# The next group's layer norm and step sizes beside the state steps, its denominators at the head of the pairs

## The reference, cut to what matters

```python
proj = x @ W_in.T
z, xc, dt_raw, bc = jnp.split(proj, ...)
dt = jnp.clip(jax.nn.softplus(dt_raw + dt_bias), DT_MIN, DT_MAX)
def step(carry, inp):
    y, v = carry
    denom = 1.0 + dt_t[:, :, None] * kdamp + dt_t[:, :, None] ** 2 * A
    v = (v - dt4 * A * y + dt4 * u_t * Bv_t) / denom
    y = y + dt4 * v + dt4 * u_t * By_t
    o = einsum(y, Cy_t) + einsum(v, Cv_t)
```

## Time and profile before

| what | us |
|---|---|
| median of three runs | 531.29 |
| the profiled execution, its own time | 531.18 |
| its span in the trace | 529.4 |
| matrices and steps of group 1, fills included | 139.6 to 190.2 |
| its pairs and what overlaps them | 190.3 to 242.8 |
| its tail | 242.8 to 260.4 |

### The profile page before, as it was taken

One profiled execution on the slowest core, in us unless ns is written; L12 is line 12 of the kernel. 1 busy time (PEld: TensorE's weight loads), 2 busy tenths in 40 slices (PEclk: granted clock), 3 DMA queues, 4 the chain that ended last, 5 costly groups with the idle time before them and its releaser, 6 DMA issues.

```text
span 529.4 us, 9508 instructions
## 1 busy us (share of the span) xinstructions
PE 446.4 (84%) x3185; PEld 344.8 (65%) x3185; DVE 445.4 (84%) x1268; ACT 242.6 (46%) x482; POOL 282.7 (53%) x367
## 2 busy tenths in 40 slices
PE   6980159996989989997889969898789969998997
PEld 5360158774756667675757659676656658876986
DVE  7699988968999999968999998968889998787542
ACT  1522227443475436442575526443466534343463
POOL 2007887656108876657108686567305776777000
PEclk9686559999999979999999988999899998998999
DMA  7500000200000001200000000110000000000000
GB/s 221 169 1 0 1 1 2 81 2 1 0 1 1 1 1 43 80 2 2 1 0 2 0 2 21 47 36 2 1 0 2 1 1 22 1 2 1 1 11 11
DMA packets 14794, 10.23 MB, mean 19 GB/s; under 512 B 1797, under 2 KB 13966, under 8 KB 14618
## 3 DMA queue, kind: packets, MB, share of 16 engines
q1 hardware_dynamic: 14746, 9.63, 6.2%
HBM read 8.55 MB, written 1.07 MB: 18 GB/s over the span
## 4 chain that ended last, share of the span: by engine, by line
DVE 41%; PE 37%; POOL 9%; issue 8%; ACT 3%; DMA 1%; SPq 0%; DVEq 0%; POOLq 0%; ACTq 0%
PE BC L612 6%; DVE tpA L1291 6%; DVE GV L1291 5%; DVE xr L1439 5%; PE HB L515 4%; DVE BC L1302 4%; PE GV L634 4%; POOL vt L1628 3%; PE HB L572 3%; PE HB L504 3%; POOL rinv L1663 2%; DVE mm L1339 2%; DVE GV L1302 2%; PE HB L622 2%; PE OO L693 2%
## 5 line engine op out<-in xcount | busy, mean ns | idle before, releaser
L612 PE MATMUL BC<-xnT,winT 128*128 128x128 f32 x512 | 78.8, 303 | 40.7 <-ACT pr L926 22.8
L612 PEld LDWEIGHTS BC<-xnT,winT 128*128 128x128 f32 x512 | 69.3, 211 | 54.1 <-issue 28.9
L1625 POOL TENSOR_TENSOR big<-mm 128x256 f32<-128x256 f32 x64 | 50.2, 784 | 52.3 <-DVE mm L1339 45.7
L1648 POOL TENSOR_SCALAR uT<-uT,skipT 128x512 f32<-128x512 f32 x8 | 12.5, 1570 | 89.3 <-DVE w L1424 53.9
L564 PE MATMUL HB<-xnT,w 128*128 128x512 f32 x108 | 52.0, 603 | 3.7 <-ACT gtm L1013 2.1
L1628 POOL TENSOR_TENSOR vt<-mm 128x256 f32<-128x256 f32 x64 | 53.9, 842 | 0.0
L634 PE MATMUL GV<-big,vt 128*128 128x128 f32 x256 | 44.0, 296 | 8.9 <-POOL vt L1628 8.9
L1637 POOL TENSOR_TENSOR mm<-ab,pr 128x256 f32<-128x256 f32 x48 | 41.4, 884 | 14.9 <-ACT pr L926 14.9
L950 ACT ACTIVATE big<-GV 128x256 f32<-128x256 f32 x60 | 23.1, 384 | 56.8 <-PE GV L637 55.5
L1337 DVE TENSOR_TENSOR mm<-BC,pr 128x512 f32<-128x512 f32 x64 | 44.2, 691 | 5.7
L634 PEld LDWEIGHTS GV<-big,vt 128*128 128x128 f32 x256 | 35.4, 200 | 16.8 <-POOL vt L1628 13.6
(11 more groups left out here) (212 smaller groups left out, 1117.1 us busy)
## 6 DMA issues: line engine op xcount, KB each, us to landing
ab<-dt_rows SPq DMA_DIRECT2D x12, 256.0 KB, 4.2
xr<-in_x SPq DMA_DIRECT2D x4, 256.0 KB, 4.9
winT<-in_w_inT SPq DMA_DIRECT2D x1, 1024.0 KB, 6.5
w<-in_rw SPq DMA_DIRECT2D x1, 1024.0 KB
out<-xr SPq DMA_DIRECT2D x3, 256.0 KB, 3.0
taps<-in_dw_wT SPq DMA_DIRECT2D x1, 512.0 KB, 3.8
w<-in_sw SPq DMA_DIRECT2D x2, 128.0 KB
out<-xr SPq DMA_DIRECT2D x2, 128.0 KB, 1.8
```

Of the source, the lines that this page charges most:

```text
L612: last = pe.matmul(b[:, j * TS:(j + 1) * TS], winT[:, col:col + NS], xt, start=True, stop=True)
L1625: pool.tensor_tensor(wt[q % 8][:], m[:, 0], m[:, 3], ALU.add)
```

## The change

Nothing is computed otherwise. Of the next group's front:

- The layer norm's statistics go from iteration 0 to slots 0 to 6 between the steps (`S_STATS`, `S_AGGR`, `S_EPS`), and `scale_and_shift` to the head of POOL's `fills`, in groups 1 and 2 ahead of `skip_gate`.
- The norm is applied on ACT after expert 2, transposed by PE after `hidden` of expert 3, ahead of `expert_out` of expert 2 (`XN_AFTER`, `XNT_AFTER`), and the logits stand after `hidden` of expert 4. ACT's exponential `step_exp`, with its table load, stands behind conversion 5.
- The logits' two DVE operations are in slots 32 and 34 and the twelve of the series in slots 52 to 63; the first of them waits for the exponential.
- PE's rows and ACT's copy of them stand before iteration 0, and the denominators in iterations 0, 1, 2 and 4.
- The running sums stand in iterations 11 and 12, the exponentials after 17 and 18, beta in 18, alpha in 20.
- For group 1, whose front lies beside the steps of group 0, ACT's parts stand between its conversions.

```diff
-F_INV, F_BETA, F_DEN, F_ALPHA = KP + 2, KP + 3, KP + 3, KP + 5
+F_INV, F_BETA, F_DEN, F_ALPHA = KP + 1, KP + 2, KP + 2, KP + 4
...
+F_DENS, DENS_AT = (9, 10, 12, 13), (0, 1, 2, 4)
+SCANS_AT = (11, 12)
+S_STATS, S_AGGR, S_EPS, S_LOGITS, S_DT = 0, 4, 6, 32, 52
+XN_AFTER, XNT_AFTER, LOGITS_AFTER = 2, 3, 4
+DT_OPS = 12
...
             for g in range(NG):
+                if g + 1 < NG:
+                    rows_of_dt(g + 1)
                 for k in range(STEPS_OF[g]):
...
-                        front_early(g + 1, k)
+                        if k in DENS_AT:
+                            denominator(g + 1, DENS_AT.index(k))
...
                         hidden(g, e)
+                        if g + 2 < NG:
+                            if e == XNT_AFTER:
+                                norm_T(LN1, g + 2)
+                            if e == LOGITS_AFTER:
+                                logits(g + 2)
                         if e:
                             expert_out(g, e - 1)
...
             for g in range(NG):
+                if g + 1 < NG:
+                    rows_copy(g + 1)
                 for k in range(STEPS_OF[g]):
...
                             if e == last:
                                 convert(g + 1, n)
+                                if n == 5 and g + 2 < NG:
+                                    step_exp(g + 2)
+                        if g + 2 < NG:
+                            if e == XN_AFTER:
+                                norm1(g + 2)
+                            if e == XNT_AFTER:
+                                xnT_copy(g + 2)
+                            if e == LOGITS_AFTER:
+                                logits_copy(g + 2)
...
+            def front_stage(g, slot):
+
+                if S_STATS <= slot < S_STATS + GT:
+                    c = slot - S_STATS
+                    if c == 0:
+                        dve.wait_ge(ld_x[g], 16)
+                        dve.wait_ge(ln_xn, ln_index(LN1, g))
+                    ins = dve.bn_stats(stats[:, c, :], xr[g % 3][:, c, :])
...
+                n = slot - S_DT
+                if n == 0:
+                    dve.wait_ge(dt_exp, g + 1)
+                    chained(dve.tensor_scalar(le, le, E_MAX, None, ALU.min))
...
             def fills(g):
-                skip_gate(g)
+                if g == 0:
+                    skip_gate(g)
+                if g + 1 < NG:
+                    scale_and_shift(ln_index(LN1, g + 1))
+                if g:
+                    skip_gate(g)
```

221 lines of the change are left out of this document (147 added, 74 removed).

## The result

The changed kernel takes **571.5 us** (median of six runs, 568.0 to 575.9) against 531.3 for the kernel before: a ratio of 1.074, 95% interval 1.068 to 1.080. I had predicted 535.2 with a range to 540. The sign was the likeliest one, the size was wrong by 36 us. The profiled execution took 573.24 us, with a span of 571.4 where the one before had 529.4: 42.0 us to be explained. (One execution of one experiment, e5_beta, took 876 us, and TensorE's products of 128x512 lasted 1148 ns in it where they last 610 in the kernel after; it is used for nothing else.)

What follows compares the result with a forecast made beforehand. DVE was taken to set the pace beside the steps, with the front costing the pairs about 6 us. Steps 11.4, pairs 0 to 8 -9.6, pairs 8 to 15 3.1, tails -0.9: +4.0 on 531.18, 535.2 us, range 527.8 to 540.

Steps and rivals of the forecast that it cites:

- the tail: Behind the last pair: DVE loses work, ACT's exponentials and beta come in the way; -0.3 us in each of three groups.
- pairs 0 to 8: First half of the pairs: statistics and series leave DVE, denominators come to PE; -1.1, -4.1 and -4.4 us, together -9.6.
- if the pairs win under 2 us per group: One of the signs, named beforehand, that would show the forecast to be wrong.
- Slot 52: Steps of groups 1 and 2: DVE waits 3.3 us for ACT's exponential, at full cost.
- DVE's own work: Steps of groups 1 and 2: statistics 1.3 us, one logit operation 0.1, six series operations 0.6; +2.0 us.
- costs about 0.1 in a filled slot: Steps: price of a small DVE operation in a filled slot; in an empty slot it costs nothing.
- PE's delay in the steps: Steps: PE waits for a bank and is 3.1 us late, then 3.9; the expert additions on DVE do not wait further.
- Head of the pairs: Ahead of pair 0: the rows' path takes 8.2 us, DVE's last fills end at 9.0; cost nothing at full clock.
- the front costs about 6 us in the first half: Pairs 0 to 8 take 25.3 us in group 1, 19.1 in group 3 without a front; the difference can be won.
- the half-clock rival: Head of the pairs: PE at half clock; 538.5 us with one such group, 541 with two; 0.16 with the third rival.
- the next one: Third rival: running sums in iterations 11 and 12 hold POOL and PE up by up to 2 us each; 539 us.
- Pairs 8 to 15: Second half of the pairs: denominators and rows leave PE, two running sums come to DVE; 1.5, 0.8 and 0.8 us, together +3.1.

Runs made afterwards that it cites:

- e5_beta: The changed kernel with beta and alpha one iteration later, as before the change, and the exponentials left early: 566.9 us, ratio 1.065.
- s2_series: The changed kernel with denominators, running sums, their exponentials, beta and alpha put back in the iterations of before: 544.9 us, ratio 1.022.
- d2_early: d1_stats with norm, transposes, logits, exponential, series and rows two iterations earlier in the pairs: 541.9 us, ratio 1.017.
- s3_dens: The changed kernel with running sums, their exponentials, beta and alpha put back in the iterations of before; denominators stay early: 547.5 us, ratio 1.026.
- s4_scans: The changed kernel with only the exponentials of the sums, beta and alpha one iteration later, as before the change: 554.2 us, ratio 1.039.
- d1_stats: The kernel before with only the next group's statistics in empty slots between the steps and POOL's scale and shift behind its first fill: 531.1 us, ratio 0.999.

## Why the prediction was wrong

The two stages that were furthest off are the tail (-0.9 forecast, +10.9 measured) and pairs 0 to 8 (-9.6 and +0.7). The prediction had named "if the pairs win under 2 us per group" as a sign of being wrong, and it came: they won 0.7 and 1.7 in groups 1 and 2 and lost 3.0 in group 0.

**Slot 52: right.** Predicted 3.3 us, measured 3.31 and 3.27, by the path that was worked out: bank, norm, GELUs, conversion 5, table load. "DVE's own work" of 2.0 us was near too as far as the statistics go (1.3 forecast; the first four steps take 5.55 us for 4.59, so 1.0).

**A small operation "costs about 0.1 in a filled slot": wrong.** That price came from the reciprocal in the earlier trace rows, which runs when POOL is idle. The series stands where POOL fills. Its cost beside the wait was 1.4 us, not 0.6, and 5.6 us for one operation in group 0, where I had reckoned 0.3. The evidence was among my own rows: the first operation of the series lasts 0.66 us at 90.34 in the earlier trace rows, for a tile of 128x16, and elsewhere in the kernel before:

```profile
211.72 0.73 DVE L1160 TENSOR_SCALAR tfs<-tfs 128x16 f32<-128x16 f32 x1
...
211.69 0.73 POOL L1625 TENSOR_TENSOR big<-mm 128x256 f32<-128x256 f32 x1 [1.15 <-DVE mm L1339]
```

It ends with POOL's operation, 0.03 us apart. The rows show that such a DVE operation waits for POOL. The Trainium skill, page "SBUF — State Buffer", section "Who interferes with whom", says that a DVE instruction in a two-port mode contends with GpSimd, and one with two SBUF inputs with a GpSimd instruction that reads SBUF, and that the one that issues second is blocked until the first has finished. The 0.66 and 0.73 us agree with that; the 5.60 us of group 0 go beyond it, since there the block outlasts the seven POOL instructions that began behind it.

**PE's delay in the steps: half priced.** I had PE 3.1 us late with no effect on DVE. It was 2.7 us late (`expert_out` begins 9.76 us after the first step, not 7.04), but its next 3 us ran at half clock, and DVE waited 1.5 us more for it in group 1. In group 2 the clock was full there, and that did not happen.

**Head of the pairs: free at full clock alone.** The path that I put 0.8 us inside DVE's last fills held in group 1. In group 2 it ran at half clock, and DVE waited 1.96 us for ACT's square ahead of the first pair, the +1.9 in the fills' line.

**Pairs 0 to 8, -9.6: the wrong reading.** The stretch itself shortened by more than I said once the front was gone (s2_series: -4.2, -5.1, -6.6). But "the front costs about 6 us in the first half", from group 3's 19.1 us in the earlier trace rows, was no gain to be had: the next stretch became longer by 3.7, 3.2 and 3.2 us at once. In the kernel before, pair 7 to 8 takes 5.8 us (the series) and pair 8 to 9 takes 2.1. In group 3 they take 1.9 and 4.8. A wait for the tail's work sits there in either case, and the series lay under it. From pair 0 to 15 taking the front away is worth 0.4, 1.9 and 3.4 us. The d2_early kernel shows the other side of it: the series taken out from under that wait costs 4.9, 2.3 and 3.7 us from pair 0 to 15, for about 4 us of work.

**The denominators at the head** then cost 1.9, 4.5 and 2.5 us of pairs 0 to 8 and gave 3.5 back behind (s3_dens against s2_series). In group 1 that is the half-clock rival, which I had at 0.16 together with the next one.

**Pairs 8 to 15, +3.1: too little.** Three parts: +3.7, +3.2 and +3.2 us from the wait that came back (s2_series), -3.5 from the denominators gone (s3_dens), and +3.1 to +4.0 from the sums (s4_scans): 2.84 us each, with PE's `gv` waiting for `vt` (1.66 us behind the second one in group 1). The sums cost less than the 4.4 us of DVE that I had booked. Missing in the sum is the wait, the same error as in the stretch ahead of it.

**The tail, -0.9: the step that failed most.** The gain was real and larger (s4_scans -1.0 to -3.1 against s3_dens). Both causes of the loss stood in the text, "ACT's first pair of exponentials ... stands ahead of the copy of the norms" and beta over `ubar`, and 0.4 us "later than now" was all that was booked for them. The first alone is 1.9 us, two rows of 1.05 us, and nothing hid it, because the norms, POOL's `rinv`, `du` and `ub` and PE's product are one chain. It brought beta onto `du` (1.7 us), and behind PE's waits of 5 us the rest ran at half clock (1.8 us: from the start of L690 to PE's first product of the next group, 4.13 us against 2.33 in s4_scans). Together 5.4, and the tails differ by 5.6 (`ub` itself takes 1.12 us for 0.93). I had let the exponentials' length be absorbed by slack that the rows of before do not have: there `rinv` begins 6.4 us behind the last products, here 8.5.

**The clock, left out of the sum.** It was one rival for one place. The kernel before, in its 17 executions beside d1_stats and d2_early, took 527.7 us at a mean granted clock of 0.942 and 535.5 at 0.920, so 8 us hang on about 24 us more of half clock (twice the difference in clock, times the length). An estimate from that for the 58 us more of half clock in the kernel after is 20 us, half of the loss. I read these 20 us not as a further cause but as what PE's new waits were multiplied by: in the tail of group 1, 3.6 us of waiting came out as 5.4. No experiment separates the two over the whole kernel.
